# Loops over batches and groups written out as straight code on all engines

## What is computed

```python
x = x + attention(layernorm(x), Wq, Wk, Wv, Wo, q_norm_w, k_norm_w)
x = x + lora_mixture(layernorm(x), A, B, Wr, br)
# attention: 32 query heads, 8 key/value heads, head size 128
q, k, v = heads(x @ Wq.T), heads(x @ Wk.T), heads(x @ Wv.T)
q, k = rmsnorm(q) * q_norm_w, rmsnorm(k) * k_norm_w
p = softmax(q @ k.T / sqrt(128) + alibi_bias_causal)
out = (p @ v) @ Wo.T
```

## Time and profile before

| | |
|---|---|
| median of 3 runs | 2344.05 us (2343.06 to 2346.43) |
| span of the profiled execution | 2337.8 us; its own time is not listed, the median is 6.25 us longer than the span |
| TensorE busy | 2204.3 us, 94% |
| VectorE, ScalarE, GpSimd busy | 1403.3, 1185.4 and 912.3 us |
| mean granted TensorE clock | 0.975 |
| packets of the two instruction queues | 138 on q8 (2.26 MB), 32 on q14 (0.25 MB) |

### The profile page before, as it was taken

How to read it: one execution, slowest core, us unless ns; L and a number is a source line. 1 busy time by engine, 2 the same in 40 slices (tenths; PEclk the granted TensorE clock), 3 DMA queues, 4 the chain that set the end, 5 groups by cost and what they waited for, 6 DMA issues and landing times.

```text
span 2337.8 us, 39513 instructions
## 1 busy us (share of the span) xinstructions
PE 2204.3 (94%) x12540; PEld 1901.5 (81%) x12540; DVE 1403.3 (60%) x3492; ACT 1185.4 (51%) x3397; POOL 912.3 (39%) x912
## 2 busy tenths in 40 slices
PE   6999999999999999999869999999999999999997
PEld 5887888878788887888668878787887888878885
DVE  4655656656565655656656556565565656656666
ACT  3554545555454555645235556454554545555552
POOL 3344343434343343444124434334343343434341
PEclk9999999999999999999989999999999999999999
DMA  3001010010101001010120010100001010010000
GB/s 118 19 1 46 1 46 1 13 34 1 46 1 43 4 1 46 1 46 1 47 67 7 1 46 1 47 1 28 19 1 46 1 46 1 1 46 1 1 1 37
DMA packets 27914, 53.40 MB, mean 23 GB/s; under 512 B 3033, under 2 KB 3033, under 8 KB 27745
## 3 DMA queue, kind: packets, MB, share of 16 engines
q1 hardware_dynamic: 26112, 50.34, 6.5%
q10 hardware_dynamic: 1632, 0.55, 0.1%
HBM read 46.68 MB, written 4.19 MB: 22 GB/s over the span
## 4 chain that ended last, share of the span: by engine, by line
PE 83%; issue 9%; POOL 4%; DVE 1%; ACT 1%; DMA 0%; ACTq 0%; POOLq 0%; DVEq 0%
PE s_ps L863 23%; PE turn_ps L855 17%; PE o_ps L863 16%; PE q_ps L863 14%; PE y_ps L863 13%; POOL probs L612 3%; DVE pT_lo L688 1%; ACT qn L531 1%; POOL q_inv_t L583 1%; DMA bias<-in_L_ffn_B 0%; ACT pT_hi L488 0%; POOL rstd L583 0%; POOL q_sum_eps_t L581 0%; PE q_ps L1013 0%; POOL bias L622 0%
## 5 line engine op out<-in xcount | busy, mean ns | idle before, releaser
L612 POOL TENSOR_TENSOR probs<-probs,p_inv_t 128x896 f32<-128x896 f32 (+7 forms) x512 | 576.7, 1147 | 724.7 <-DVE p_inv_t L756 724.7
L488 ACT ACTIVATE pT_hi<-turn_ps 128x512 fp32r<-128x512 f32 x576 | 332.7, 600 | 487.2 <-PE turn_ps L855 486.2
L748 DVE CUSTOM_DVE_ANT_0 probs<-s_ps,bias 128x896 f32<-128x896 f32 (+7 forms) x512 | 382.2, 753 | 187.2 <-issue 184.6
L688 DVE TENSOR_TENSOR pT_lo<-turn_ps,pT_hi 128x512 fp32r<-128x512 f32 x576 | 383.3, 686 | 142.9 <-ACT pT_hi L488 139.7
L525 ACT ACTIVATE probs<-probs,neg_max 128x896 f32<-128x896 f32 (+7 forms) x512 | 396.0, 774 | 81.0 <-DVE neg_max L748 80.8
L855 PE MATMUL turn_ps<-ident,probs 128*128 128x128 f32 x2560 | 364.7, 278 | 26.3 <-POOL probs L612 9.7
L855 PEld LDWEIGHTS turn_ps<-ident,probs 128*128 128x128 f32 x2560 | 309.6, 143 | 79.6 <-issue 16.6
L863 PE MATMUL s_ps<-kT_hi,qT_lo 128*128 128x512 f32 (+3 forms) x768 | 268.3, 349 | 50.0 <-issue 50.0
L863 PE MATMUL s_ps<-kT_hi,qT_hi 128*128 128x512 f32 (+3 forms) x768 | 280.2, 365 | 0.5 <-DVE qT_lo L690 0.5
L863 PE MATMUL s_ps<-kT_lo,qT_hi 128*128 128x512 f32 (+3 forms) x768 | 265.3, 345 | 0.0
L863 PE MATMUL o_ps<-pT_hi,v_hi 128*128 128x512 f32 x576 | 250.3, 434 | 12.2 <-DVE pT_lo L688 11.8
(11 more groups left out here) (98 smaller groups left out, 3976.6 us busy)
## 6 DMA issues: line engine op xcount, KB each, us to landing
wq_raw<-in_L_attn_Wq SPq DMA_DIRECT2D x16, 1024.0 KB, 6.7
wo_raw<-in_L_attn_Wo SPq DMA_DIRECT2D x16, 1024.0 KB, 5.4
y<-in_L_attn_x SPq DMA_DIRECT2D x16, 256.0 KB, 3.7
wkv_raw<-in_L_attn_Wk SPq DMA_DIRECT2D x16, 256.0 KB, 2.9
wkv_raw<-in_L_attn_Wv SPq DMA_DIRECT2D x16, 256.0 KB, 3.8
out<-y SPq DMA_DIRECT2D x16, 256.0 KB, 2.1
bias<-in_L_ffn_A ACTq DMA_DIRECT2D x1, 256.0 KB
bias<-in_L_ffn_B ACTq DMA_DIRECT2D x1, 256.0 KB
```

Of the source, the lines that this page charges most:

```text
L488: nc.scalar.activation(target, source, ACT.Copy).then_inc(sems["hi_done"], 1)
L612: nc.gpsimd.tensor_tensor(row, row, p_inv_t[:, s % 2, h:h + 1].to_broadcast((P, L)), ALU.mult).then_inc(sems["p_ready"], 1)
L688: nc.vector.tensor_tensor(target, source, high.bitcast(F32), ALU.subtract).then_inc(sems["lo_done"], 1)
L748: nc.vector.tensor_tensor_reduce(out=probs[:, s % 2, h, 0:L], in0=s_ps[:, at_col:at_col + L], in1=bias[:, h, S - L:S], scale=-1.0, scalar= ...
```

## The change

Each loop of the machine becomes a loop of the program that writes the kernel, so that every pass is written out in full. The loop's number is then a constant, and so is each value that is waited for. Units, their order, tiles, banks and semaphores stay as they are.

```diff
@@ run_plans, all engines
-            with engine.Fori(0, NG - 1) as g:
+            for g in range(NG - 1):
                 run(GROUP, lambda name: group_at(name, b, g), lambda name: group_at(name, b, g),
                     *([g + 1] if with_group else []))
@@ SyncE
             for b in range(NB):
-                with sp.Fori(0, NG - 1) as g:
+                for g in range(NG - 1):
                     load_next(b, g, g + 1)
@@ ScalarE
-            with act.Fori(0, NB) as b:
+            for b in range(NB):
@@ GpSimd
-            with pool.Fori(0, NB) as b:
+            for b in range(NB):
@@ VectorE
-            with dve.Fori(0, NB) as b:
+            for b in range(NB):
@@ TensorE
-            with pe.Fori(0, NB) as b:
+            for b in range(NB):
```

## The result

The changed kernel takes 2247.28 us, median of 4 runs (2246.55 to 2247.54), against 2343.91 (2343.06 to 2346.43, 4 runs): ratio 0.9584, 95% interval 0.9571 to 0.9598, 4.2% faster. The forecast was 2258.5, in a range from 2249.

A forecast was written before the change was run, and what follows sets the result against it. TensorE, 94% busy, was held back by stalls at the group loop's 12 backward branches. Span 2337.8 less 84.65 there and 0.9 at the batch edge, plus 6.25 around it, gave 2258.5 us, range 2249 to 2278.

The forecast's parts named there:

- 6.25 us around the span: Whole run: time outside the profiled span, from median 2344.05 against span 2337.8, added to the forecast span of 2252.2 us.
- (2): Later bodies' head: the first body's 1.39 us wait for `qn` does not come back, so later bodies take 132.11 us.
- (5): Batch loop edge: VectorE's issue wait goes, but the last `x` load limits the gain to 0.9 us, between 0 and 2.88.
- (1): First body of a batch: without the branch's gap at its end it lasts 133.50 us.
- (3): Loop bodies: TensorE sets the pace; the stall does not let other engines catch up on work it waits for.
- (4): Group loops of both batches: straight code takes 926.16 us for either, saving 84.65 us, 7.05 per branch.
- (6): Register instructions in the bodies: costed at nothing, at most 10 us in all, from 0.71 us left over in the first body.
- registers cost something too: Rival, chance 0.08: removing register instructions wins up to 10 us more, giving 2248.5 us.
- (7): Long program: about 98 instruction blocks for TensorE and about 5 per body on other engines cost nothing.
- not the branch's but a block boundary's: Rival, chance 0.04: the 4.2 us stall near a body's head stays in straight code, nothing moves, 2344 us.
- rival of code fetches on other engines: Rival, chance 0.04: VectorE, ScalarE and GpSimd stop for 60 fetched blocks, 173 us lost, 2431 us.
- rule on 2048 instructions: TensorE's memory: by the rule the 1632-instruction body stays resident, giving 2343 us; laid aside because the trace has 9 packets.

The follow-up runs named there:

- e11: The changed kernel run again, beside the aligned-loop kernel with straight batch loops: 2247.84 us, ratio 0.9609 to the kernel before.
- e12: Kernel before with TensorE's group loop head at a block start and batch loops straight on VectorE, ScalarE and GpSimd: 2249.84 us, ratio 0.9616.
- e3: Kernel before with group loops straight on all engines, batch loops and register instructions kept: 2249.90 us, ratio 0.9617.
- e5: Kernel before with all loops kept and TensorE's group loop head aligned to the start of a 256-instruction block: 2249.23 us, ratio 0.9614.
- e2: Kernel before with both loops straight on all engines but TensorE, which keeps its loops: 2343.75 us, ratio 1.0014.
- e7: Kernel before with loops kept and TensorE's group loop head at slot 246 of a 256-instruction block: 2345.58 us, ratio 1.0024.
- e6: Kernel before with loops kept and TensorE's group loop head at slot 192 of a block, padding run through: 2302.26 us, ratio 0.9842.
- e9: Kernel before with loops kept and TensorE's group loop head at slot 136 of a block, padding jumped over: 2250.45 us, ratio 0.9618.
- e10: Kernel before with loops kept and TensorE's group loop head at slot 150 of a block, padding jumped over: 2260.83 us, ratio 0.9660.
- e4: Kernel before with the batch loop straight on all engines, group loops kept: 2305.36 us, ratio 0.9864.
- e8: Kernel before with each batch's first body straight, then three passes of two bodies, TensorE's head at slot 246: 2304.93 us, ratio 0.9847.

## Why the prediction was right in its mechanism and 11.2 us too high

The step that failed is the one that put 6.25 us around the span; the runs show 1.75 to 1.90 there (below). With 1.8 in its place the same sum gives 2254.0, and the low end of the range 2244.6, which takes in the 2247.28 measured. The other misses are of size, in the terms (2) and (5) and behind the last body.

Of the 11.2 us, 6.5 are a saving in the span that was larger than forecast (92.1 against 85.55), 4.4 the time outside the span, and 0.3 the profiled run against the median.

(1) Right: 133.50 forecast, 133.56 and 133.52 measured.

(2) The wait does not come back, as forecast, but its price was mis-sized. The rows above show `q_part.2.0` 58.25 - 54.77 = 3.48 us behind the head in the first body and 190.18 - 188.33 = 1.85 in the second, so 1.63 apart with 1.38 of idle; at `turn.q.1` it is 4.69 against 2.91, 1.78 apart. The row counts its idle time from the modelled end of the `turn` ahead (56.24 + 0.62 = 56.86); without a wait the matmul starts before that end, 0.38 us behind the start of the `turn` (189.80 to 190.18) instead of 2.01. That is 0.25 us more than the idle time, and the six matmuls up to `turn.q.1` bring another 0.15 (59.46 - 58.25 = 1.21 against 191.24 - 190.18 = 1.06). A wait of 1.38 us is worth 1.78, and later bodies are 131.77 on average, not 132.11: 12 x 0.34 = 4.1 us, the largest part of the miss in the span. The forecast took the idle time of the row alone.

(3) Right: TensorE sets the pace. The one wait for another engine that is left in a later body, 0.8 us of `o_ps` for VectorE's `pT_lo`, was there before with 0.7.

(4) 84.65 forecast, 88.66 measured; the difference is that of (2).

(5) Mis-sized: 0.9 forecast, 2.24 measured. The stretch from the last add to `normalise` fell from 8.04 us (1171.04 to 1179.08) to 5.35. The step took the end of a row of two transfers as the time when the last load is issued (and 1174.29 + 3.7 is 1178.0, not the 1177.6 of the prediction). In the changed kernel that row runs from 1127.22 to 1129.21, and the load was there by 1131.56: with the 3.7 us of the earlier trace rows to landing, it was issued by 1127.9, ahead of the row's end. The wait for the load came, as forecast, but is 0.19 us (0.36 in e11, 1.23 in e12), so this term varies by about a microsecond. Of the 2.69 won there 1.13 was lost again in the rest of the prepare plan, and the last group gave 0.68.

(6) Right, and the bound was loose: the 0.71 us left over in the first body are the wait for `pT_lo` (0.7), and nothing is left for registers. The measured time is nearest to that of the rival "registers cost something too" (2248.5), but that rival is excluded: e3 and e5 keep the register instructions and have the bodies of the straight code.

(7) Right in price; 100 packets on q8 where 98 were forecast, 63 on q14 where 90 were.

After the last body 1.23 us was won where nothing was forecast. In a window of 15 us at the same place in the program (2290.00 to 2305.00 before, 2199.10 to 2214.10 after) the granted clock was 0.77 before and 0.89 after; that the clock is the cause was not tried.

**Outside the span.** The step that set 6.25 us around the span was wrong. Each run now has its own span: 2247.54 with 2245.7, and in every run of the twelve experiments, and of the kernel before beside them, the time is 1.75 to 1.90 us above the span of the same run. The profiled execution before took therefore about 2339.6 us, not 2344.05; the kernel before varies from 2334.29 to 2346.43 in these runs, and its stalls vary (3.58 to 4.60 us in its own profile, 2.66 to 6.37 in e2's), and the shown runs lay in the upper half. A span and a median of other runs were mixed.

**The stall's cause.** The prediction put it to the branch and to two blocks fetched after it. The first half holds, and so does that TensorE stands while the second packet behind the branch comes. But not two packets come again: all nine do, on every pass, because the head lay where the body touches 8 blocks; and the stall is long because the head lay some 15 instructions ahead of a block's end. (The pages of e5, e7 and e6 count 30, 10 and 414 instructions more than that of the kernel before, so 15, 5 and 207 of padding per batch, up to the block's end, to slot 246, and to slot 192 of the next block: each gives slot 241.) The rival "not the branch's but a block boundary's" (0.04) was wrong on straight code and yet named the other half of the cause: it takes a branch and a boundary close behind its target. The rival of code fetches on other engines would show in e2 as slower; there it is 0.14% (0.05 to 0.24), and what grew is the gap ahead of TensorE's bodies, not a wait for another engine. The gap in the bodies behind a branch fits this picture in e6, e7, e9 and e10. So does e4's first batch: its stall sits nine matmuls or 1.0 us of work further on than that of the kernel before, and is 3.3 us on average where 4.2 was. How many blocks the memory keeps is not read anywhere; that it is eight is worked out from where the step lies, between 136 and 150.

**The rule on 2048 instructions.** At offsets 0 and 136 the body stays, at 150, 192 and 246 it does not. By the Trainium skill, page "Runtime: NRT & Kernel Launch", section "Instruction fetch mechanics", TensorE's memory holds 2048 instructions in blocks of 256; the prediction laid the rule aside on the evidence of nine packets. Its number agrees with the runs if whole blocks are counted, the one ahead included. The same section of the Trainium skill says that a taken branch outside a window of two pages must fetch its target, which the prediction did not weigh; on TensorE, e5's branch goes back over 7 blocks and fetches nothing, so here the measurement decides against it. The roughly 108 ns that the Trainium skill, page "Advanced Engine Details and Errata", section "Control Flow Timing", gives for a compare-and-branch do not show either: e5's bodies are no longer than straight ones. With the branch recorded 3.0 us ahead of the last matmul, such a time could not be seen there.

## What to carry to other kernels

- An issue wait right behind a backward branch, with packets on the instruction queue in every pass, is a question of where the loop's code lies. Count the loop's instructions, waits and register instructions included, and the blocks it touches, and try an aligned head before unrolling: the aligned head alone gave 3.9% (e5), and so did straight code on all engines (e11).
- A wait's price is the shift of the work behind it between two passes with and without it, not its idle time; one of 1.38 us was worth 1.78.
- Compare a span with the time of the same execution, and never with the median of others when a stall varies.

## What the runs showed that was not expected

- A loop of 1653 instructions stays on TensorE at head offset 136 (32 packets) and is fetched whole at 150 (140 packets): 14 instructions cost 10.4 us (2250.45 to 2260.83).
- The next block comes 4.8 to 6.2 us after the restart in e6 and e7; a head 246, 192 and 150 slots into its block gives stalls of about 4.8, 1.6 and 0 us, besides a gap of 0.3 to 1.0 us ahead of it.
- Padding that is run through ahead of a loop costs once per entry: 10.9 us in e6, 7.9 in e8. In e5, where it is run through too, no issue wait shows. In the traces the padding instructions start 0.07 us apart: 207 take 15.3 us in e6, 150 take 10.8 in e8, and the 15 of e5 take 1.0, which TensorE still had matmuls to cover.
